# An expert stage whose gate and up products come out turned, on one core

## The reference

```
h   = h + attention(layernorm(h))                       # 64 x 69 tokens of 256
x   = layernorm(h)                                      # 4416 x 256
top2, w = the two best of 8 experts per token, softmax of their two logits
for each expert e and each token t sent to it (8832 pairs):
    hidden = silu(x[t] @ w13[e][:, :512]) * (x[t] @ w13[e][:, 512:])    # 512
    out[t] += w[t, e] * (hidden @ w2[e])                                # 256
```

## Time and profile before

| | us |
|---|---|
| median of the runs | 874.67 |
| the profiled execution's own time | 869.38 |
| its span | 867.6 |
| expert stage, from its first gather to the end | about 495 to 867.6 |
| TensorE busy, share of the span | 725.0, 84% |
| DVE busy | 563.0, 65% |
| ACT busy | 398.1, 46% |
| POOL busy | 444.7, 51% |

### The profile page before, as it was taken

The page is one execution under the profiler, slowest core; times in us unless marked ns, Lnnn a source line. Parts: engine busy times, 40 slices in busy tenths (PEclk is TensorE's granted clock), DMA queues, the critical chain, the costliest instruction groups (busy, mean ns, idle before and its releaser), DMA issues. The chain is left out here.

```text
span 867.6 us, 27607 instructions
## 1 busy us (share of the span) xinstructions
PE 725.0 (84%) x9892; PEld 509.5 (59%) x9892; DVE 563.0 (65%) x1164; ACT 398.1 (46%) x881; POOL 444.7 (51%) x613
## 2 busy tenths in 40 slices
PE   6667889997899988889811299999999999999993
PEld 5534666766677766666600156666666666666662
DVE  6866878786888767777369645555555555555552
ACT  1233666676787767778400033333333333333331
POOL 5652544464675545553314535555555555555552
PEclk9966999999999999999555589999999999999997
DMA  8575566455355544454110013333333333333332
GB/s 266 189 227 173 170 208 197 118 158 154 121 169 157 170 138 148 132 168 136 59 16 1 13 38 54 59 63 57 56 63 57 57 63 59 55 63 57 57 62 25
DMA packets 64872, 91.80 MB, mean 106 GB/s; under 512 B 13176, under 2 KB 45704, under 8 KB 64679
## 3 DMA queue, kind: packets, MB, share of 16 engines
q1 hardware_dynamic: 49655, 66.81, 25.6%
q0 software_dynamic: 15088, 23.21, 15.6%
HBM read 58.95 MB, written 24.10 MB: 96 GB/s over the span
## 5 line engine op out<-in xcount | busy, mean ns | idle before, releaser
L1245 POOL DMA_INDIRECT out<-y,token_of x76 | 120.6, 1586 | 138.7 <-DMA out<-y,token_of 113.2
L1290 DVE SCALAR_TENSOR_TENSOR hid<-quad,up_scale,silu 128x512 f32<-128x512 f32 x76 | 57.1, 751 | 100.1 <-PE quad L1326 100.1
L1326 PE MATMUL quad<-w_hi,x_hi 128*128 x304 | 116.1, 382 | 1.1 <-DVE x_lo L1297 1.1
L1326 PE MATMUL quad<-w_lo,x_hi 128*128 x304 | 116.0, 382 | 0.0
L1326 PE MATMUL quad<-w_hi,x_lo 128*128 x304 | 116.0, 382 | 0.0
L519 DVE TENSOR_REDUCE nm_src<-quad 69x16 f32<-69x1104 f32 x64 | 82.9, 1296 | 26.4 <-PE quad L815 26.2
L1238 POOL DMA_INDIRECT xg<-xn_rows,token_of x76 | 75.6, 994 | 35.5 <-issue 25.3
L1258 ACT ACTIVATE hid_hi<-bank 128x512 f16<-128x512 f32 x76 | 45.4, 597 | 104.2 <-PE bank L1345 104.2
L703 ACT ACTIVATE probs<-quad 69x1104 f32<-69x1104 f32 x64 | 69.7, 1088 | 45.4 <-PE quad L898 45.1
L1270 ACT ACTIVATE x_hi<-bank 128x256 f16<-128x256 f32 x76 | 29.2, 384 | 120.9 <-PE bank L1366 120.9
L1326 PE MATMUL bank<-w_hi,hid_hi 128*128 x304 | 82.9, 273 | 1.6 <-ACT hid_hi L1258 1.6
(11 more groups left out here) (213 smaller groups left out, 1867.2 us busy)
## 6 DMA issues: line engine op xcount, KB each, us to landing
w_lo<-in_experts_w SPq DMA_DIRECT2D x24, 512.0 KB, 5.8
w_raw<-in_experts_w SPq DMA_DIRECT2D x48, 256.0 KB, 5.3
xt<-in_patches SPq DMA_DIRECT2D x18, 384.0 KB, 6.0
h<-h_rows SPq DMA_DIRECT2D x34, 128.0 KB, 5.0
hb<-h_rows SPq DMA_DIRECT2D x34, 128.0 KB, 5.9
out<-h SPq DMA_DIRECT2D x34, 128.0 KB, 5.3
xn_rows<-xn SPq DMA_DIRECT2D x34, 128.0 KB, 4.9
vb<-v SPq DMA_DIRECT2D x30, 138.0 KB
```

Of the source, the lines that this page charges most:

```text
L1245: nc.gpsimd.indirect_dma_start(out, bass.IndirectOffsetOnAxis(token_of[:, n:n + 1], 0), y[q][:, :], None, compute_op=ALU.add).then_inc(add ...
L1290: nc.vector.scalar_tensor_tensor(out=hid[q][:, :], in0=quad[:, 2 * q + 1, :], scalar=up_scale[:, :], in1=silu[q][:, :], op0=ALU.mult, op1= ...
L1326: last = nc.tensor.matmul(dst, x[:, k, :], w[:, bass.ds(col + k * (2 * width if width == HIDDEN else width), width)], start=(k == 0 and m ...
```

## The change

The gate and up products change sides. A 128x128 piece of weights becomes the stationary side and 128 columns of the turned x the moving side, so the result has hidden units in its rows, as the last product wants them. The four transposes of `hid` and their semaphore `hid_turned` go, and PSUM bank `b4` is no longer used in this stage. Gate and up are then 4 x 2 x 3 matmuls of 128 columns each, 48 for both instead of 12 of 512 columns. `x_hi` and `x_lo` lie in one buffer `x_parts`. `hid_hi` and `hid_lo` are now made from `hid` in SBUF in the same step as `hid`, before `y` of the tile ahead. TensorE's step now is: gate of tile t, transposes of x of tile t+1, up of tile t, load of the next expert number, last product of tile t-1. POOL's list is unchanged.

```diff
@@ scalar @@
-                            n, q, half, on, has = part(t - 1)
-                            if on:
-                                act.wait_ge(s["hid_turned"], n + 1)
-                                if has(-2):
-                                    act.wait_ge(s["y_mm"], n - 1)
-                                nc.scalar.activation(hid_hi[q][:, :, :].rearrange("p c n -> p (c n)"), b4[:, :], ACT.Copy).then_inc(s["hid_hi_ready"], 1)
                             n, q, half, on, has = part(t)
...
-                                nc.scalar.activation(x_hi[q][:, :, :].rearrange("p c n -> p (c n)"), b5[:, 0:DIM], ACT.Copy).then_inc(s["x_hi_ready"], 1)
+                                nc.scalar.activation(x_parts[q][:, :, 0, :], b5[:, 0:DIM].rearrange("p (c n) -> p c n", n=P), ACT.Copy).then_inc(s["x_hi_ready"], 1)
+                            n, q, half, on, has = part(t)
+                            if on:
+                                act.wait_ge(s["hid_ready"], n + 1)
+                                if has(-2):
+                                    act.wait_ge(s["y_mm"], n - 1)
+                                nc.scalar.activation(hid_hi[q][:, :, :].rearrange("p c n -> p (c n)"), hid[q][:, :], ACT.Copy).then_inc(s["hid_hi_ready"], 1)
@@ vector: x_lo of t+1 now first, hid_lo of t right behind hid of t @@
+                                nc.vector.tensor_tensor(x_parts[q][:, :, 1, :], b5[:, 0:DIM].rearrange("p (c n) -> p c n", n=P),
+                                                        x_parts[q][:, :, 0, :], ALU.subtract).then_inc(s["x_lo_ready"], 1)
...
+                                nc.vector.tensor_tensor(hid_lo[q][:, :, :].rearrange("p c n -> p (c n)"), hid[q][:, :],
+                                                        hid_hi[q][:, :, :].rearrange("p c n -> p (c n)"), ALU.subtract).then_inc(s["hid_lo_ready"], 1)
@@ tensor @@
+                        def turned(dst, x, col):
+                            for c in range(KH):
+                                for k in range(KD):
+                                    at = bass.ds(col + k * 2 * HIDDEN + c * P, P)
+                                    place = dst[:, c * P:(c + 1) * P]
+                                    nc.tensor.matmul(place, w_lo[:, at], x[:, k, 0, :], start=(c == 0 and k == 0), stop=False, skip_group_check=True)
+                                    nc.tensor.matmul(place, w_hi[:, at], x[:, k, 0, :], start=False, stop=False, skip_group_check=True)
+                                    last = nc.tensor.matmul(place, w_hi[:, at], x[:, k, 1, :], start=False, stop=(c == KH - 1 and k == KD - 1), skip_group_check=True)
+                            return last
...
-                                for k in range(KH):
-                                    last = nc.tensor.transpose(b4[:, k * P:(k + 1) * P], hid[q][:, k * P:(k + 1) * P], idt[:, :])
-                                last.then_inc(s["hid_turned"], 1)
...
-                                terms(quad[:, 2 * q, :], x_hi[q], x_lo[q], KD, expert[n] * W_EXPERT, HIDDEN).then_inc(s["gate_mm"], 1)
-                                terms(quad[:, 2 * q + 1, :], x_hi[q], x_lo[q], KD, expert[n] * W_EXPERT + HIDDEN,
-                                      HIDDEN).then_inc(s["up_mm"], 1)
+                                turned(quad[:, 2 * q, :], x_parts[q], expert[n] * W_EXPERT).then_inc(s["gate_mm"], 1)
...  (transposes of x of t+1, as before)
+                                turned(quad[:, 2 * q + 1, :], x_parts[q], expert[n] * W_EXPERT + HIDDEN).then_inc(s["up_mm"], 1)
```

More of the change, by code:

```diff
@@ L1208, in experts @@
                 xg = ring("xg", [P, DIM + EXPERTS])
-                x_hi, x_lo = ring("x_hi", [P, KD, P], fp16), ring("x_lo", [P, KD, P], fp16)
+                x_parts = ring("x_parts", [P, KD, 2, P], fp16)
                 silu, hid, y = ring("silu", [P, HIDDEN]), ring("hid", [P, HIDDEN]), ring("y", [P, DIM])
@@ L1275, in step @@
                         def step(t):
-                            n, q, half, on, has = part(t - 1)
+                            n, q, half, on, has = part(t + 1)
                             if on:
-                                dve.wait_ge(s["hid_hi_ready"], n + 1)
+                                dve.wait_ge(s["x_hi_ready"], n + 1)
                                 if has(-2):
-                                    dve.wait_ge(s["y_mm"], n - 1)
-                                nc.vector.tensor_tensor(hid_lo[q][:, :, :].rearrange("p c n -> p (c n)"), b4[:, :],
-                                                        hid_hi[q][:, :, :].rearrange("p c n -> p (c n)"), ALU.subtract).then_inc(s["hid_lo_ready"], 1)
+                                    dve.wait_ge(s["up_mm"], n - 1)
+                                nc.vector.tensor_tensor(x_parts[q][:, :, 1, :], b5[:, 0:DIM].rearrange("p (c n) -> p c n", n=P),
+                                                        x_parts[q][:, :, 0, :], ALU.subtract).then_inc(s["x_lo_ready"], 1)
                             n, q, half, on, has = part(t)
@@ L1288, in step @@
                                 if has(-2):
-                                    dve.wait_ge(s["hid_turned"], n - 1)
+                                    dve.wait_ge(s["hid_lo_ready"], n - 1)
                                 nc.vector.scalar_tensor_tensor(out=hid[q][:, :], in0=quad[:, 2 * q + 1, :], scalar=up_scale[:, :], in1=silu[q][:, :],
                                                                op0=ALU.mult, op1=ALU.mult).then_inc(s["hid_ready"], 1)
-                            n, q, half, on, has = part(t + 1)
+                            n, q, half, on, has = part(t)
                             if on:
-                                dve.wait_ge(s["x_hi_ready"], n + 1)
+                                dve.wait_ge(s["hid_hi_ready"], n + 1)
                                 if has(-2):
-                                    dve.wait_ge(s["up_mm"], n - 1)
-                                nc.vector.tensor_tensor(x_lo[q][:, :, :].rearrange("p c n -> p (c n)"), b5[:, 0:DIM],
-                                                        x_hi[q][:, :, :].rearrange("p c n -> p (c n)"), ALU.subtract).then_inc(s["x_lo_ready"], 1)
+                                    dve.wait_ge(s["y_mm"], n - 1)
+                                nc.vector.tensor_tensor(hid_lo[q][:, :, :].rearrange("p c n -> p (c n)"), hid[q][:, :],
+                                                        hid_hi[q][:, :, :].rearrange("p c n -> p (c n)"), ALU.subtract).then_inc(s["hid_lo_ready"], 1)
                             n, q, half, on, has = part(t - 1)
@@ L1325, in terms @@
                                 for m, (x, w) in enumerate(((hi, w_hi), (hi, w_lo), (lo, w_hi))):
-                                    last = nc.tensor.matmul(dst, x[:, k, :], w[:, bass.ds(col + k * (2 * width if width == HIDDEN else width), width)],
+                                    last = nc.tensor.matmul(dst, x[:, k, :], w[:, bass.ds(col + k * width, width)],
                                                             start=(k == 0 and m == 0), stop=(k == chunks - 1 and m == 2))
@@ L1352, in step @@
                                 if has(-2):
-                                    pe.wait_ge(s["hid_ready"], n - 1)
-                                terms(quad[:, 2 * q, :], x_hi[q], x_lo[q], KD, expert[n] * W_EXPERT, HIDDEN).then_inc(s["gate_mm"], 1)
-                                terms(quad[:, 2 * q + 1, :], x_hi[q], x_lo[q], KD, expert[n] * W_EXPERT + HIDDEN,
-                                      HIDDEN).then_inc(s["up_mm"], 1)
-                                if has(1):
-                                    load_expert(n + 1)
+                                    pe.wait_ge(s["silu_ready"], n - 1)
+                                turned(quad[:, 2 * q, :], x_parts[q], expert[n] * W_EXPERT).then_inc(s["gate_mm"], 1)
                             n, q, half, on, has = part(t + 1)
@@ L1367, in step @@
                                 last.then_inc(s["x_turned"], 1)
+                            n, q, half, on, has = part(t)
+                            if on:
+                                if has(-2):
+                                    pe.wait_ge(s["hid_ready"], n - 1)
+                                turned(quad[:, 2 * q + 1, :], x_parts[q], expert[n] * W_EXPERT + HIDDEN).then_inc(s["up_mm"], 1)
+                                if has(1):
+                                    load_expert(n + 1)
                             n, q, half, on, has = part(t - 1)
```

2 lines of the change are left out of this document (1 added, 1 removed).

## The result

The changed kernel takes 977.01 us (median of four runs, 971.49 to 979.91) against 874.64 for the kernel before (now median of four, 872.46 to 876.48): a ratio of 1.1179, 95% interval 1.1119 to 1.1239. It is slower by about 102 us. The profiled execution took 979.61 us, its trace spans 977.8.

What follows compares the result with a forecast made beforehand. TensorE and serial scatters bound the kernel; the change makes TensorE's sequencer the bound: 4.8 + 0.7 + 0.4 = 5.9 us a tile. First scatter 512.5 + 436.6 + 4.5 + 9.0 gives span 962.6, forecast 967 us, range 935 to 997 (80%).

Steps and rivals of the forecast that it cites:

- The bound before: Expert stage of the kernel before: TensorE at 4.55 us a tile and serial scatters at about 4.5 to 4.64 bind together.
- The sequencer as the new bound: Expert stage after the change: TensorE's sequencer making addresses sets the pace, over TensorE's own 4.1 us and the scatters' 4.64.
- The price per tile: Expert stage, changed kernel: 5.9 us a tile from groups, expert-number load, waits and transposes of x; ends 5.6 and 6.25.
- the term of 20 groups at 0.24: TensorE's sequencer: 16 gate and up groups plus 4 of the last product, 0.24 us each, 4.8 us a tile.
- The start of the stage: Expert stage's beginning: first gate matmul at 499.72 as before, first scatter at 512.5 instead of 510.94.
- From the profiled execution to the median: End of the sum: median was 5.3 us above the profiled execution; half added to 964.4, giving 967 us.
- A sign that did not come: List by line: TensorE's idle time put down to issue would be large at the new gate and up matmul lines.
- Serial weight loads: Rival, gate and up on TensorE: loads strictly one after another at 0.098 us, 6.2 us a tile, 989 us; chance 5%.
- the pair price of 0.08: Rival, gate and up: a load and matmul pair costs 0.08 us on the engine, 5.4 us a tile, 930 us; chance 6%.
- The clock: Rival, expert stage: TensorE's clock drops to 0.50, so 8.2 us a tile and 1137 us; chance 2%.
- The two rivals in which addresses are free: Expert stage, TensorE ahead: scatters back to back at 4.5 us, 865 us, chance 4%; or still 4.64, 874 us, chance 3%.
- the later y is a shift once and no price per tile: DVE: y behind hid_lo comes about 1.4 us later; POOL and the scatter wait, once, with no cost per tile.

Runs made afterwards that it cites:

- e6: Kernel before with the accumulating scatter replaced by a plain DMA store to scratch rows, waiting for none before it: 859.88 us, ratio 0.9836.
- e1: Changed kernel with gate and up always at the columns of expert 0, so without register operations there: 908.31 us, ratio 1.0413 to the kernel before.
- e4: Changed kernel with w_hi in place of w_lo in gate and up, so a group's three matmuls share one address: 892.81 us, ratio 1.0266 to the kernel before.
- e3: Kernel before with each 512-column gate and up matmul cut into four of 128 columns, each group at its own column position: 985.4 us, ratio 1.1348.
- e2: Kernel before with gate and up always at the columns of expert 0, so without 8 of its 16 register operations a tile: 872.14 us, ratio 1.002.
- e9: Changed kernel with real addresses and y of the tile before placed ahead of hid_lo on DVE: 977.31 us, 1.1192 times the kernel before.
- e5: e1 with the accumulating scatter replaced by a plain DMA store to scratch rows, waiting for none before it: 844.15 us, ratio 0.9667 to the kernel before.

## Why the prediction was right, point by point

- **The bound before.** Right. With the scatters out (e6) the kernel before gains only 1.6%: TensorE at 4.55 us stands right behind them.
- **The sequencer as the new bound.** Right, and shown from both sides: taking away its operations (e1, e4) takes away most of the loss, adding them to the kernel before (e3) makes the loss without a change of sides, and taking them from where they were hidden (e2) does nothing.
- **The price per tile.** Forecast 5.9 us, measured 6.05. The step that was a little small is the term of 20 groups at 0.24: undisturbed they take the 0.23 of the rows above, but now and then a group is late (at 704.57 in the timeline above the next one starts only at 704.85 and not at 704.80), and 6.05 less 0.7 and 0.4 leaves 0.25 a group. The starts of the register operations in the trace say the same (540 to 940 us, gate and up, last product): median distances 0.124 and 0.113, so 0.237 a group, but about one in eight is late by 0.015 to 0.17, and the mean group is 0.252. What makes them late is not shown. 74 x 0.15 are 11 of the 15 us by which the span is over the forecast of 962.6.
- **The start of the stage.** The first gate matmul came at 504.38, not 499.72; the parts in front, which are not changed, took 4.7 us longer in this execution. From it to the first scatter were 12.2 us against the 12.8 of my sum. So 11.1 + 4.7 - 0.6 = 15.2.
- **From the profiled execution to the median.** I had added half of 5.3 us. Here the profiled execution was 2.6 us above the median instead. This is chance, and it helped: the profiled execution missed its forecast of 964.4 by 15 us, the median missed 967 by only 10. With the half added as forecast, the median would have been 982, still in the range. The 0.2% that the prediction took as the least change to be told was too fine: the interval of the ratio reaches 0.6% to each side.
- **A sign that did not come.** I had said that the idle time put down to issue would be large at the new matmul lines. The list by line, 540 to 940 us, has it at the last product alone:

```profile
L1327 PE MATMUL quad<-x_parts,w_lo 128*128 128x128 f16 x1060 | 225.4, 225 | 0.2
L1335 PE MATMUL bank<-w_hi,hid_hi 128*128 x264 | 72.5, 275 | 41.8 <-issue 41.8
```

  A matmul is listed with 0.22 us, longer than the 0.11 it waits for its address, so the list sees no idle time there. The distances of starts show the bound, the idle column does not.
- **Serial weight loads, and the pair price of 0.08.** Both rivals fall: 0.055 us between gate matmuls in e1 and in the changed kernel where the sequencer is ahead. The Trainium skill's 81 ns for a pair at 128 columns ("TensorE: Matmul & The Clock Gate", Back-to-back issue gap) is not what the engine does here; 0.08 comes out only where the sequencer's 0.24 is shared by three.
- **The clock.** It was at 1.00 from 510 to 960 us, rival refuted.
- **The two rivals in which addresses are free.** The forecast did not need them, but their times were wrong. I gave 865 to 874 us for a TensorE that is ahead; e1 shows 908. The step "the later y is a shift once and no price per tile" holds at 6.05 us (e9) and fails below about 5.1: I had followed the wait from `y` to the scatter but not on from the scatter through the gather behind it back to TensorE.

## What to carry to other kernels

Count distinct run-time addresses, not only matmuls: with an operand that moves by a register, a group of matmuls costs its engine's columns or its sequencer's operations, whichever is more, and here splitting 512 columns into four by 128 turned 0.65 us of columns per 0.24 of sequencer into 0.17 per 0.24. The sequencer's operations stand in the trace by line, so their distance can be read before the change, where they are still hidden. When one bound is so far above the others that it hides every reordering, look for the next one by following each wait round until it comes back to its own engine.

## What the runs showed of the hardware

- Register operations of TensorE's sequencer are about 0.12 us apart when it is not held up, whether one, two or three pairs of load and matmul stand between them (e4: three pairs and one operation, 0.13; the changed kernel: three pairs and two, 0.23).
- A stream of 128x128 fp16 weight loads, each with one matmul of 128 columns, keeps 0.055 us a pair at the full clock, although each load is listed with 96 to 99 ns.
- An operand addressed by a register costs about the same as the stationary side and as the moving side (changed kernel 6.05 us a tile; e3 6.2 with four transposes more).
- The parts in front of the expert stage are the same in all kernels, yet its first gather starts at 495.0 us in the trace of the kernel before, 499.6 in that of the changed one, 488.0 in e3 and 502.4 in e5. So spans of single executions are compared stage by stage.
